# Perceiver layer on one core: the running row sums of cross-attention split between VectorE and GpSimd

## The reference

```python
q = proj(layernorm(x), Wq, bq)          # 16 heads, 256 x 32
k, v = proj(ctx, Wk, bk), proj(ctx, Wv, bv)   # 16 heads, 4096 x 32
scores = clip(q @ k.T / sqrt(32), -50, 50)
scores = clip(where(attend, scores, -10000), -50, 50)
probs = softmax(scores)                 # over the 4096 keys
ctx = probs @ v
```

## Time and profile before

| | us |
|---|---|
| median of 3 runs (716.7 to 716.88) | 716.76 |
| the profiled execution, its own time | 716.85 |
| its span in the trace | 714.7 |
| TensorE matmuls busy | 699.3 (98%) |
| VectorE busy | 610.2 (85%) |
| ScalarE busy | 435.5 (61%) |
| GpSimd busy | 11.6 (2%) |
| first exp of cross-attention to the first of the last block | 35.03 to 278.27 |

### The profile page before, as it was taken

One profiled execution on the slowest core, in us unless ns is written; L12 is line 12 of the kernel. 1 busy time (PEld: TensorE's weight loads), 2 busy tenths in 40 slices (PEclk: granted clock), 3 DMA queues, 4 the chain that ended last, 5 costly groups with the idle time before them and its releaser, 6 DMA issues.

```text
span 714.7 us, 20508 instructions
## 1 busy us (share of the span) xinstructions
PE 699.3 (98%) x8722; PEld 455.1 (64%) x8722; DVE 610.2 (85%) x946; ACT 435.5 (61%) x598; POOL 11.6 (2%) x36
## 2 busy tenths in 40 slices
PE   8999999999999998998999999999999999999998
PEld 3555555555555554546777767777777777777775
DVE  5689999999999999787889977888888888888885
ACT  4778888787878886735677753444444344444442
POOL 3000000000000000010000000000000000000000
PEclk9999999999999999999999999999999999999999
DMA  8560101010110000032334403667677776767770
GB/s 322 174 276 3 62 3 62 6 58 14 50 30 36 2 3 3 2 138 87 112 122 155 161 1 103 226 216 249 221 245 227 238 235 231 244 223 244 223 244 32
DMA packets 29880, 94.44 MB, mean 132 GB/s; under 512 B 5824, under 2 KB 15088, under 8 KB 28400
## 3 DMA queue, kind: packets, MB, share of 16 engines
q1 hardware_dynamic: 28944, 92.31, 38.7%
q10 hardware_dynamic: 864, 1.07, 0.5%
HBM read 92.76 MB, written 0.57 MB: 131 GB/s over the span
## 4 chain that ended last, share of the span: by engine, by line
PE 62%; DVE 29%; ACT 4%; issue 4%; DMA 1%; POOL 0%; DVEq 0%; ACTq 0%
PE pS L1227 35%; PE pP L1227 12%; PE pD L1227 8%; DVE arena L898 7%; PE pO L1227 5%; DVE x_sb L907 4%; DVE arena L907 4%; DVE xT L907 4%; DVE xn L907 3%; DVE arena L758 2%; DVE arena L764 2%; ACT arena L566 2%; DMA arena<-in_ctxT 1%; ACT arena L527 1%; PE pO L1622 1%
## 5 line engine op out<-in xcount | busy, mean ns | idle before, releaser
L1227 PE MATMUL pS<-arena 128*128 128x256 f16 (+3 forms) x2185 | 253.5, 272 | 1.9 <-ACT arena L591 0.8
L1227 PEld LDWEIGHTS pS<-arena 128*128 128x128 f16 (+1 forms) x2185 | 213.1, 101 | 46.0 <-ACT arena L623 1.9
L1227 PE MATMUL pP<-arena 128*32 128x512 f16 (+1 forms) x2996 | 239.8, 380 | 0.7 <-ACT arena L467 0.7
L1227 PEld LDWEIGHTS pP<-arena 128*32 128x32 f16 (+1 forms) x2996 | 109.1, 97 | 102.0 <-issue 2.2
L527 ACT ACTIVATE arena<-pS,mblk 128x1024 f32<-128x1024 f32 x112 | 128.9, 1206 | 4.9 <-PE pS L1227 4.7
L1053 DVE SCALAR_TENSOR_TENSOR arena<-arena 128x1536 f16<-128x1536 f32 x72 | 126.1, 1752 | 0.8 <-ACT arena L667 0.8
L707 ACT ACTIVATE arena<-pS 128x256 f32<-128x256 f32 x72 | 27.7, 384 | 154.1 <-PE pS L1227 154.1
L1227 PE MATMUL pO<-arena 128*32 128x256 f32 (+6 forms) x1370 | 106.8, 357 | 2.6 <-DVE arena L1048 2.0
L667 ACT ACTIVATE arena<-arena 128x1536 f16<-128x1536 f32 x72 | 106.4, 1477 | 1.0 <-PE pP L1227 1.0
L898 DVE TENSOR_SCALAR arena<-arena 128x1024 f32<-128x1024 f32 x112 | 73.3, 689 | 7.4 <-ACT arena L527 7.4
L1227 PE MATMUL pD<-arena 128*128 128x512 f16 x288 | 77.8, 379 | 0.0
(11 more groups left out here) (252 smaller groups left out, 520.0 us busy)
## 6 DMA issues: line engine op xcount, KB each, us to landing
arena<-in_units SPq DMA_DIRECT2D x72, 768.0 KB, 4.7
arena<-w_scratch SPq DMA_DIRECT2D x136, 64.0 KB, 2.7
arena<-in_ctxT SPq DMA_DIRECT2D x7, 1024.0 KB, 5.2
mw_in<-in_mla_in SPq DMA_DIRECT2D x8, 832.0 KB, 7.0
mw_out<-in_mla_out SPq DMA_DIRECT2D x8, 512.0 KB, 3.6
wlatT<-in_wlatT SPq DMA_DIRECT2D x1, 1280.0 KB, 10.7
arena<-in_ctxT ACTq DMA_DIRECT2D x4, 256.0 KB, 6.1
arena<-in_wkT SPq DMA_DIRECT2D x4, 256.0 KB, 5.7
```

Of the source, the lines that this page charges most:

```text
L1227: return pe.matmul(o, lhsT, rhs, start=start, stop=stop, **kw)
```

## The change

In blocks 0 to 6 the first slot of a pair (even tile) is still added by VectorE, the second (odd tile) by GpSimd, into the same running sum. In block 0, where a group's first two tiles are added to each other by one instruction, that stays on VectorE. So VectorE has one addition for each pair, 56 in all, and GpSimd 52 (8 for each of blocks 1 to 6 and 4 in block 0). Since both add into one tensor, they take turns: GpSimd waits for VectorE's addition of the pair, and VectorE's next addition to the same group waits for GpSimd's. The one semaphore `sum_done` becomes `first_added` and `second_added`, and the exps and `add_sums` wait on whichever applies.

```diff
-def adds_until(b, g, tile):
-
-    before = sum(3 if i == 0 else 4 for i in range(NBLK - 1) for j in range(HC) if (i, j) < (b, g))
-    return before + (max(1, tile) if b == 0 else tile + 1)
+def firsts_until(b, i):
+
+    return PAIRS_X * b + i + 1
+
+
+def seconds_until(b, i):
+
+    return (i + 1) // 2 if b == 0 else PAIRS_X * b - HC + i + 1
...
+            def add_second(b, i):
+
+                g, t = i // 2, 2 * (i % 2) + 1
+                pool.wait_ge(s["clip_done"], STEPS * b + CT * g + t + 1)
+                pool.wait_ge(s["first_added"], firsts_until(b, i))
+                pool.tensor_tensor(psums[g], psums[g], probs[:, t], ALU.add).then_inc(s["second_added"], 1)
+
+            for b in range(NBLK - 1):
+                for i in range(PAIRS_X):
+                    if b or i % 2:
+                        add_second(b, i)
...
-                            act.wait_ge(s["sum_done"], adds_until(b, g - 1, tile) if g else adds_until(b - 1, HC - 1, tile))
+                            slot = (b, i - 2) if g else (b - 1, PAIRS_X + i - 2)
+                            if tile % 2 == 0 or slot[0] == 0 and slot[1] % 2 == 0:
+                                act.wait_ge(s["first_added"], firsts_until(*slot))
+                            else:
+                                act.wait_ge(s["second_added"], seconds_until(*slot))
...
-                        for t in (tile, tile + 1):
-                            dve.wait_ge(s["clip_done"], STEPS * b + CT * g + t + 1)
-                            dve.wait_ge(s["sum_done"], adds_until(b, g, t) - 1)
-                            dve.tensor_tensor(acc, acc, probs[:, t], ALU.add).then_inc(s["sum_done"], 1)
+                        dve.wait_ge(s["clip_done"], STEPS * b + CT * g + tile + 1)
+                        if tile == 0:
+                            dve.wait_ge(s["second_added"], seconds_until(b - 1, 2 * g + 1))
+                        elif not first:
+                            dve.wait_ge(s["second_added"], seconds_until(b, 2 * g))
+                        else:
+                            dve.wait_ge(s["first_added"], firsts_until(b, 2 * g))
+                        dve.tensor_tensor(acc, acc, probs[:, tile], ALU.add).then_inc(s["first_added"], 1)
...
-                pe.wait_ge(s["sum_done"], adds_until(b, g, CT - 1))
+                pe.wait_ge(s["second_added"], seconds_until(b, 2 * g + 1))
```

More of the change, by code:

```diff
@@ L247, in build @@
             ctx_hi ctx_lo proj_done proj_evac k_lo
-            scores_done exp_done clip_done pv_done sum_done dsum_done
+            scores_done exp_done clip_done pv_done first_added second_added dsum_done
             last_pv den_read inverted rows_done ctx_mul ctxn_ready delta_done
@@ L564, in last_block @@
                         if i < 2:
-                            act.wait_ge(s["sum_done"], adds_until(b - 1, HC - 1, tile))
+                            if tile % 2 == 0:
+                                act.wait_ge(s["first_added"], firsts_until(b - 1, PAIRS_X + i - 2))
+                            else:
+                                act.wait_ge(s["second_added"], seconds_until(b - 1, PAIRS_X + i - 2))
                         act.activation(probs[:, tile], step_scores(st), ACT.Exp,
@@ L901, in x_block @@
                         dve.wait_ge(s["clip_done"], STEPS * b + 2 * i + 2)
-                        dve.tensor_tensor(acc, probs[:, 0], probs[:, 1], ALU.add).then_inc(s["sum_done"], 1)
+                        dve.tensor_tensor(acc, probs[:, 0], probs[:, 1], ALU.add).then_inc(s["first_added"], 1)
                     else:
-                        for t in (tile, tile + 1):
-                            dve.wait_ge(s["clip_done"], STEPS * b + CT * g + t + 1)
-                            dve.wait_ge(s["sum_done"], adds_until(b, g, t) - 1)
-                            dve.tensor_tensor(acc, acc, probs[:, t], ALU.add).then_inc(s["sum_done"], 1)
+                        dve.wait_ge(s["clip_done"], STEPS * b + CT * g + tile + 1)
[3 more added lines that the diff above has]
+                            dve.wait_ge(s["second_added"], seconds_until(b, 2 * g))
+                        else:
+                            dve.wait_ge(s["first_added"], firsts_until(b, 2 * g))
+                        dve.tensor_tensor(acc, acc, probs[:, tile], ALU.add).then_inc(s["first_added"], 1)
                     if split and i >= HC:
```

## The result

The changed kernel takes 757.04 us (median of 4 runs, 756.04 to 757.84) against 716.79 for the kernel before: 1.056 times as long, 95% interval 1.0547 to 1.0572, or 40.2 us more. The forecast was 762.8, with a range of 722 to 795. The span of its profiled execution is 754.2 us, 39.5 more than before.

What follows compares the result with a forecast made beforehand. TensorE was taken to bound the blocks, VectorE in a tie. Added: 0 in block 0, 31.2 us in blocks 1 to 4, 7.7 in block 5, 7.1 in block 6; 716.85 + 46.0 = 762.8 us, range 722 to 795.

Steps and rivals of the forecast that it cites:

- TensorE's floor: Cross-attention blocks: TensorE needs 4.36 us a pair of key tiles, 34.9 us a block, which relieving VectorE cannot shorten.
- The gain: Seam to the last block: relieving VectorE saves at most 1 us, 0.36 of it a TensorE wait for a clip.
- GpSimd's price: Each GpSimd addition of 1024 columns takes 2.47 us, worked out from selects with two inputs read one after the other.
- The lower price of 2.25 us: GpSimd addition: half the skill's 4497 ns for 2048 columns; using it would take 11 us off the forecast.
- Exclusion: Loop pairs: GpSimd instructions that read SBUF and VectorE's work exclude each other, leaving 2.20 us a pair uncovered.
- the overlap of 0.27: Each pair: 0.21 us of VectorE's start under GpSimd's end and 0.06 the other way, credited against GpSimd's addition.
- What leaves VectorE: Blocks 1 to 6: eight additions of 1.23 us leave VectorE, 9.84 us a block; four leave in block 0.
- Block 1: Forecast like blocks 2 to 4: 42.65 us against 34.86, 7.79 us more.
- Block 6 and the seam: First exp of block 6 to that of the last block: 7.1 us more than 34.26; last block unchanged.
- Overlap: Rival: GpSimd's reads don't stop VectorE, so TensorE keeps 4.36 us a pair; 715.8 to 717 us, chance 0.12.
- Waits and hand-overs: Rival: hand-overs or locks lengthen the loop, 4.8 us for each 0.1 us a pair; above 788 us, chance 0.09.
- The break-even of 1.50 us: Rival of a short GpSimd addition: up to this length TensorE's block hides it; 1.5 to 1.9 gives 717 to 737, chance 0.12.

Runs made afterwards that it cites:

- the run with every other pair: The changed kernel with GpSimd adding only each group's last tile, 28 additions instead of 52, VectorE adding the rest: 736.11 us, ratio 1.0269.

## Why the prediction was right

**TensorE's floor: right.** With VectorE relieved and nothing put in its way a block stays at 34.85 us (the run without second additions). The chain through VectorE in the earlier trace rows was a tie. The gain was bounded at 1 us and is 1.3, with an interval that takes in 1.

**GpSimd's price: right, a little high.** 2.47 us were taken. The first two additions, in block 0, ran with little in their way and took 2.38; in the loop they take 2.68, and the 0.30 more falls to VectorE's split, of which 0.38 us were left when they began (127.41 to 127.79). The price was worked out from a select of another kind, at 2.27 ns a column for two inputs and 0.147 us fixed. With the 1.28 us of a half addition the measured one is 2.15 ns a column and 0.18 us, so the reading of two inputs that come one after the other fits. The lower price of 2.25 us, which the prediction named beside its own, was 0.13 below the 2.38; the sum by it, 752, would have missed by 5 us as the forecast's 762.8 did by 6.

**Exclusion: right.** It was read off four small cases of the earlier trace rows, and 2.20 us a pair that nothing covers came out as 2.16. That the two are so close is in part luck: the price was 0.09 too high and the overlap of 0.27 was 0.05 too high (2.38 - 2.16 = 0.22), and one is taken from the other. The run with additions that nobody waits for and two inputs gives the same 2.16 with no hand-over in it.

**What leaves VectorE: wrong by 0.10 us a pair.** The sum took half of two additions' 2.46 us, 1.23. The addition that stays takes 1.13 from start to start, so the one that went had cost 1.33, as it had to wait for the first one's result. Eight times 0.10 is 0.8, and with 0.3 for the 0.04 of the exclusion it accounts, within 0.1, for the 1.0 us by which a block was forecast too long (42.65 against 41.67).

**Block 1: too high by 2.9.** It takes 4.85 us more, not 7.79; blocks 2 to 4 take 6.8 more. The missing 1.9 us is a lead that was left out: in block 0 TensorE set the pace and VectorE had slack, so block 1 used up the slots in hand before each wait for VectorE cost TensorE time. The trace after shows it: the first exps of block 1 start at 69.34, 74.08 and 78.44 us, near TensorE's 4.36 apart; TensorE waits for a clip for the first time before 78.80, and from 83.83 on the exps are some 5.1 apart.

**Block 6 and the seam: too low by 1.0, as the sum of two errors.** From the mask load of block 6 to the third exps of the last block it is 276.82 to 325.74, 48.92 us, against 245.25 to 286.09, 40.84: 8.1 more, where 7.1 were forecast. Between the marks that the forecast used, the first exp of block 6 and that of the last block, it is 275.59 to 315.58, 39.99 us against 34.26: 5.7 more, so 1.4 less than forecast. From there to the third exps it is 10.16 us against 7.82, 2.3 more in a block that the forecast called unchanged. There VectorE still had the last clips of block 6 to make, beside GpSimd's last additions. The split of latent weights at 309.03 was held by GpSimd too, for 2.85 us in place of 0.69. Some of the 8.1 is TensorE's clock, which the forecast only named as possible. The busy table of the kernel after at the seam:

```profile
309.00:313.00 4.00, 2.22 (x52) 0.98 (x44) 4.00 (x5) 2.79 (x3) 2.32 (x1) 1.00 0.00 0
313.00:317.00 4.00, 3.54 (x44) 1.14 (x40) 4.00 (x4) 1.31 (x2) 2.64 (x1) 0.57 0.02 4
317.00:321.00 4.00, 3.27 (x64) 1.55 (x64) 4.00 (x4) 1.84 (x2) 2.17 (x2) 1.00 0.00 0
```

TensorE had waited 1.78 us for a clip before 312.53, and from 313 to 317 the granted clock is 0.57, most of it at 1.2 instead of 2.4 GHz. The 24 score matmuls at 314.06 took 1.47 us, not 0.83, and the next weighing of 8 1.08 instead of 0.64. That is 1.1 us, if it all lies on the path; how much of it does was not measured.

The terms add up: -0.4 for an earlier start, 0 in block 0, 4.85, 6.79, 6.82, 6.82, 6.69 and 8.08 are 39.65 us, against 39.5 in the span.

**The rivals.** Overlap is excluded by the four runs in which GpSimd adds beside VectorE. Waits and hand-overs cost nothing that can be measured in the blocks (2.16 us a pair with and without them), and one wait of 0.27 us at the seam. The break-even of 1.50 us for an addition was not tried with whole additions of that length; half additions, of which the shortest took 1.28 us and most 1.79, still lost 26 us, but there VectorE does the other half.

## What to carry to other kernels

Work moved from a full VectorE to GpSimd is worth something only if what it frees is more than the time that GpSimd's instruction keeps VectorE waiting: here it freed 1.33 us and cost 1.99 or 2.16, at the two places in the pair that were tried. Whether two engines exclude each other is to be seen in a trace where they meet for even a microsecond, by comparing an instruction's duration there with the same shape alone. And before relieving a busy engine, leave its work out altogether and time that: here that gave the ceiling, 1.3 us, with one run.

## What was not expected

An addition by GpSimd of one tile to itself takes 2.27 us and costs VectorE 0.46 us less than one with two different inputs (2.7 us). How the reads differ can't be seen in these runs, but a stand-in for measuring contention has to have the inputs of the real instruction.

52 memsets of 0.95 us by GpSimd beside VectorE's two-input additions cost nothing that can be measured (717.25 us against 716.67, interval of the ratio 0.9997 to 1.0016), in a kernel in which VectorE has no time to spare.

A GpSimd addition that starts 0.22 us into VectorE's split goes before VectorE's next instruction in the changed kernel (127.41). In the run with every other pair one that starts 0.23 us into the split (118.70) was, by its rows, put off behind three more instructions of VectorE. What decides it stays open.
